# Moving the issue of six stores per chunk from SyncE to ScalarE in a fused convolution, state-space and mixture-of-experts kernel

## The chip, the cores and the metric

The kernel runs on one core of one Trainium2 chip. The time is device microseconds for one execution of the whole program; the lower the better. Six engines share the work: TensorE (PE, with PEld for its weight loads), VectorE (DVE), ScalarE (ACT), GpSimd (POOL) and SyncE (SP). In the kernel before, SP does nothing but issue transfers. All engines run their own instruction streams in order and meet at semaphores.

## The reference

The input is eight images of 56 x 56 tokens with 64 channels.

```python
# 1. a convolution in 32 paths of width 4
h = relu(bn1(x @ W1 + B1)); h = relu(bn2(conv3x3(h, W2) + B2)); h = relu(bn3(h @ W3 + B3))
x = relu(h.sum(paths) + x);  t = tokens(x)
# 2. a state-space layer over the tokens, forwards and backwards
s = layernorm(t);  xn = layernorm(s) * gamma + beta
#    for each direction:
xs, z = split(xn @ in_proj); xs = silu(conv4(xs)); dt = softplus(xs @ x_proj @ dt_proj + b)
h[t] = exp(dt * A) * h[t-1] + dt * B * xs;  y = (C . h + D * xs) * silu(z) @ out_proj
t = t + s + y_fwd + y_bwd
# 3. eight experts, the best two of each token, of a 64-256-64 MLP
s = layernorm(t);  t = t + moe(s, top_k=2)
```

## The kernel before

**Tiling.** An image is cut into seven chunks of 448 tokens (eight rows). The state-space layer takes each chunk twice, once in each direction, so an image has 14 steps. A step has 16 slots, one for each state (DS = 16), and the whole kernel is one loop over slots n on every engine. In slot n, PE spreads the n-th input of the recurrence into a bank (line 683), VectorE weighs it by B and runs the scan (lines 1008, 1018), GpSimd multiplies by C (line 1172), and PE gathers (line 695). ScalarE makes the decays `dtb` by an Exp (dA, line 854), up to six slots ahead (AHEAD = 6); the first of a step waits for the transfer that spreads `dt` over the partitions.

**Order.** The other two layers are woven into these slots by tables of offsets. The convolution of a chunk has a slot CONV and stages at offsets of A_AT and F_AT; the experts of a chunk have a slot TOKENS and offsets of E_AT. For all images but the first, CONV is 8 modulo 16 and comes every 32 slots, that is every second step. On each engine the order of a slot is fixed by the order of its loop body. PE and its evictors share two banks in a ring; ScalarE takes most of them in `take`.

**The chain of the step size dt.** GpSimd finishes softplus in `soft_dt` (line 1193). SP stores the result in `put_dt` (line 543, slot 5 of the step) and reads it back spread over the partitions in four transfers `spread_dt` (line 550), of which the first waits for the store. The scan of the next step needs them.

**The six stores.** `keep_rows` (line 584) stores a chunk of the first layer's rows; `put` (line 604) stores the second layer's output as three bf16 parts, one call each; `keep_xn` (line 620) stores the normed tokens in two calls. That makes one, three and two issues, six per chunk and 336 for all 56 chunks. The load `arrange` (line 613, three transfers) reads all three parts back as `h3` and must wait until they have landed (semaphore `bounced`). What is stored is made by ScalarE: `h1s` at line 869, the first part at 875, the other two in `split_h2` at 937, `xns` at 888.

**Where the slots fall.** With CONV = 8 modulo 16, the second layer is evicted and its first part stored in slot 14 of a step; in the next step part two is split in slot 1 and stored in slot 2, part three is split in slot 3 and stored in slot 4, and `arrange` also stands in slot 4, ahead of `put_dt` in slot 5. `keep_xn` of the chunk before stands in slot 1. The experts' first layer ("up", Gelu, line 896) fills slots 8 to 11 of one step and 0 to 3 of the next. In those slots ScalarE makes no decays, so that the activation table isn't changed; it makes up for them in the slot after:

```python
if not bursting and not silu:
    decays_to(n + AHEAD)      # first in the slot's body
```

Of the kernel before, what the change touches and what calls it, by code (L numbers as in the profile page):

```python
# [19 lines left out]
ROWS = 8  # L20
# [39 lines left out]
END = NB * G  # L60
DOWN_AT = (4, 7, 12, 15)
PAIR_AT = (4, 6, 12, 13)
A_AT = {"cut": -16, "second": -11, "put0": -10, "rem1": -10, "split1": -7, "put1": -6, "rem2": -8,
        "split2": -5, "put2": -4, "arrange": -4, "z": 6, "x_in": 10, "paths": 14, "mean": 15, "square": 17, "var": 17,
# [17 lines left out]
def build(nc, T):  # L82
    ctx = ExitStack()
    with ctx:
# [335 lines left out]
        def first_half(k):  # L420
            return 0 <= k + 2 < LAST

        def second_half(k):
            return 0 <= k + 1 < LAST
# [15 lines left out]
        for r in range(NB):  # L440
            for q in range(NCH):
                for what, at in A_AT.items():
                    slots["A", what, (r, q)] = G * r + CONV[a_class(r)][q] + at
                for what, at in F_AT.items():
                    slots["A", what, (r, q)] = G * r + ROWS_IN[a_class(r)][q] + at
                for j in range(ZP):
                    slots["A", "third", ((r, q), j)] = G * r + CONV[a_class(r)][q] + j * 11 // ZP
                for m in range(len(ACT_J) + 1):
                    slots["A", "z_T", ((r, q), m)] = G * r + CONV[a_class(r)][q] + A_AT["z"] + m
                t = G * r + TOKENS[e_class(r)][q]  # L450
                for what, at in E_AT.items():
                    slots["E", what, (r, q)] = t + at
                for m in range(MT):
                    slots["E", "up", ((r, q), m)] = t + EXPERTS + (m // 2 if m < 8 else 4 + m // 2)
# [31 lines left out]
        RING += [(DS * k + 11, 1, "z", k + 1, "act") for k in range(-1, LAST - 1)]  # L486
# [20 lines left out]
        for k in range(-2, LAST):  # L507
            if second_half(k):
                MISC += [(DS * k + 4, "bb", k + 1), (DS * k + 6, "cc", k + 1)]
            if first_half(k):  # L510
                MISC += [(DS * k + 12, "x", k + 2), (DS * k + 15, "dt", k + 2)]
# [26 lines left out]
        with nc.Block() as block:  # L538
            @block.sync
            def _(sp_):  # L540
# [40 lines left out]
                def keep_rows(it):  # L581
                    after(r_act, taken("paths_in", it))
                    a = (1 + F_ORD[it[1]] * ROWS) * PW
                    sp_.dma_start(h1_dram[:, a:a + ROWS * PW], h1s[:, :, :].rearrange("p r w -> p (r w)"))\
                       .then_inc(h1_out, 16)

# [11 lines left out]
                def put(it, a):  # L598
                    if a == 0:
                        after(r_act, taken("second", it))  # L600
                        after(h3_in, 48 * upto("A", "arrange", back(it, 2)))
                    else:
                        after(h2_mid, upto("A", "split1", it) + upto("A", "split2", it if a == 2 else back(it)))
                    sp_.dma_start(T["h2_scratch"][side(it), a].rearrange("c t n -> t c n"), h2p[:, a, :])\
                       .then_inc(bounced, 16)

# [9 lines left out]
                def keep_xn(it):  # L616
                    after(r_act, taken("norm_T", it))
                    for h in range(2):
                        at = A_ORD[it[1]] * CH + 3 - h
                        sp_.dma_start(xn_dram[it[0] % 2][C * h:C * h + C, at:at + CH],  # L620
                                      xns[C * h:C * h + C, :]).then_inc(xn_out, 16)

# [6 lines left out]
                for n in SLOTS:  # L629
                    k, i = n // DS, n % DS  # L630
                    if i == 4 and first_half(k):
                        fetch_xw(k + 2)
                    if i == 5 and second_half(k):
                        put_dt(k + 1)
                    for j in range(3):
                        if i == (7, 9, 13)[j] and second_half(k):
                            spread_dt(k + 1, j)
                    if i == 1 and 0 <= k < LAST:
                        spread_dt(k, 3)
# [28 lines left out]
            def _(pe):  # L668
# [16 lines left out]

                def gather_y(b):
                    k, j = b // 4, b % 4
                    if j == 0:
                        if k:
                            pe.wait_ge(o_rd, k)  # L690
                        MM(ps[YB][:, 0:CH], skip[k % 2][:, :], u[:, k % 2, :], start=True, stop=False,
                           skip_group_check=True)
# [128 lines left out]
                for n in SLOTS:  # L821
                    k, i = n // DS, n % DS
# [6 lines left out]
                    if i == 3 and 1 <= k <= LAST:  # L829
                        gather_y(4 * k - 1)  # L830
                    if i == 6 and 1 <= k <= LAST:
                        out_proj(k - 1)
                    if i in (9, 11, 15) and 0 <= k < LAST:
                        gather_y(4 * k + (9, 11, 15).index(i))
# [6 lines left out]
            def _(act):  # L841
# [19 lines left out]
                def take(what, of):  # L861
# [15 lines left out]
                    elif what == "third":  # L877
                        it, j = of
                        n, m = len(ACT_J), ACT_J.index(j)
                        gg = (upto("A", "z", it) - 1) * n + m - 4  # L880
# [23 lines left out]
                    last.then_inc(r_act, 1)  # L904

# [48 lines left out]
                for n in SLOTS:  # L954
                    k, i = n // DS, n % DS
                    bursting = any(n - ago in starts for ago in range(4))
                    silu = i == 12 and (first_half(k) or second_half(k))
# [8 lines left out]
                    if silu and first_half(k):  # L966
                        silu_u(k + 2)
# [13 lines left out]
                    if i == 5 and second_half(k):  # L981
                        copy_bb(k + 1)
                    if i == 7 and second_half(k):
                        copy_cc(k + 1)
                    if i == 15 and first_half(k):
                        soft_in(k + 2)

            @block.vector
            def _(dve):
# [42 lines left out]
                def rectify(it, j):  # L1032
                    m, a = DVE_J.index(j), acc[:, :]
                    z = bank_of("third", (it, j))[:, 0:CH]
                    if m == 0:
                        after(z_T, (len(ACT_J) + 1) * (upto("A", "z", it) - 1))
# [7 lines left out]
                def paths_out(it):  # L1044
# [3 lines left out]
                    dve.wait_ge(z_T, (len(ACT_J) + 1) * upto("A", "z", it))  # L1048
# [64 lines left out]
                for n in SLOTS:  # L1113
                    k, i = n // DS, n % DS
# [4 lines left out]
                    if i == 3 and 1 <= k <= LAST:  # L1119
                        gate(k - 1)  # L1120
                    if i == 6 and 1 <= k <= LAST:
                        add_out(k - 1)
# [29 lines left out]
            def _(pool):  # L1152
# [119 lines left out]
                for n in SLOTS:  # L1272
                    k, i = n // DS, n % DS
                    if 0 <= n < END:
                        by_c(n)
                        if i % 2 == 1:
                            keep_states(n)
                    if second_half(k):
                        if i == 0:
                            soft_le(k + 1)  # L1280
                        if i == 1:
                            soft_ym(k + 1)
                        if i == 2:
                            soft_log(k + 1)
                        if i == 3:
                            soft_dt(k + 1)
                        if i in (4, 5, 6):
                            part(k + 1, i - 4)
# [104 lines left out]
```

## Time and profile before

| | |
|---|---|
| median of 3 runs | 5047.22 us (5043.57 to 5048.93) |
| profiled execution | 5048.39 us, span 5046.6 us |
| busy: PE, DVE, POOL, ACT | 4298.5, 4019.9, 3923.8, 3319.4 us |
| bytes moved by DMA | 623.07 MB, mean 123 GB/s |
| granted TensorE clock, mean | 0.953 |

The span is from the first to the last instruction; the execution's own time is 1.8 us longer. No engine is busy all the time; the share of each is an average over slots with different limits.

### The profile page before, as it was taken

The numbers are of one execution on the slowest core, as the hardware profiler recorded it, in microseconds if no ns is written. First come the engines' busy times: TensorE is split into PE (matmuls) and PEld (weight loads), VectorE is DVE, ScalarE is ACT, GpSimd is POOL, SyncE is SP. The second block draws the span as 40 slices with busy tenths as digits, with TensorE's granted clock in tenths as the row PEclk, the third lists the DMA queues.
The fourth block names the chain that finished last, engine by engine and source line by source line (L and its number), as shares of the span: only waits on it lengthen the run. The fifth ranks groups of instructions, "written<-read, shape, count | busy, mean of one in ns | idle before, by whom it ended". The sixth has DMA issues, their size and how long they took to land.

```text
span 5046.6 us, 70047 instructions
## 1 busy us (share of the span) xinstructions
PE 4298.5 (85%) x21206; PEld 1758.3 (35%) x21206; DVE 4019.9 (80%) x6065; ACT 3319.4 (66%) x5396; POOL 3923.8 (78%) x4938
## 2 busy tenths in 40 slices
PE   3577788889898888888889898989898889888887
PEld 1233333333333333333333333333333333332332
DVE  2278888788887888888888888888888888888772
ACT  1265566667676667777776777767676767676675
POOL 1277788788887788888887888888888888888872
PEclk8688999999999999999999999999999999999998
DMA  2275655555555555555555555555555556554430
GB/s 66 66 163 135 142 131 129 134 129 134 126 132 125 130 132 129 132 137 130 139 128 134 132 136 131 132 134 133 131 137 131 131 129 136 133 123 110 98 75 5
DMA packets 255531, 623.07 MB, mean 123 GB/s; under 512 B 105268, under 2 KB 170676, under 8 KB 255028
## 3 DMA queue, kind: packets, MB, share of 16 engines
q1 hardware_dynamic: 255156, 618.60, 52.9%
q8 instruction: 171, 2.80, 0.3%
q14 instruction: 204, 1.67, 0.1%
HBM read 540.85 MB, written 77.65 MB: 123 GB/s over the span
## 4 chain that ended last, share of the span: by engine, by line
PE 33%; ACT 16%; POOL 16%; DVE 12%; issue 11%; DMA 10%; DVEq 0%; SPq 0%; ACTq 0%; POOLq 0%
PE ps L683 7%; POOL hc L1172 6%; ACT dtb L854 6%; DVE hs L1018 5%; DMA dtb<-dt_scratch 5%; PE ps L746 5%; PE ps L695 4%; DVE ps L1008 4%; DMA dt_scratch<-sp 3%; ACT L969 3%; PE ps L817 2%; PE ps L740 2%; ACT hg L896 2%; POOL sp L1185 2%; PE ps L772 2%
## 5 line engine op out<-in xcount | busy, mean ns | idle before, releaser
L1172 POOL TENSOR_TENSOR hc<-hs,cb 128x448 f32<-128x448 f32 x1792 | 2031.3, 1137 | 644.7 <-DVE hs L1018 620.6
L1018 DVE TENSOR_TENSOR_SCAN hs<-dtb,state,ps 128x448 f32<-128x448 f32 x1536 | 1755.1, 1143 | 91.2 <-DVE ps L1008 2.0
L1008 DVE TENSOR_TENSOR ps<-ps,bb 128x448 f32<-128x448 f32 x1792 | 1098.9, 613 | 427.7 <-PE ps L683 420.8
L854 ACT ACTIVATE dtb<-dtb,decay 128x448 f32<-128x448 f32 x1792 | 1087.6, 658 | 190.6 <-DMA dtb<-dt_scratch 189.2
L683 PE MATMUL ps<-dux,pick 128*128 128x448 bf16 x3584 | 1039.3, 371 | 113.0 <-DVE hs L1018 107.7
L896 ACT ACTIVATE hg<-ps,be 128x448 f32<-128x448 f32 x896 | 519.4, 631 | 411.3 <-PE ps L746 409.8
L683 PE MATMUL ps<-duz,pick 128*128 128x448 bf16 x1792 | 642.5, 359 | 0.0
L746 PE MATMUL ps<-xn,we 64*128 64x448 f32 x1792 | 564.1, 596 | 32.2 <-ACT hg L896 31.7
L683 PEld LDWEIGHTS ps<-dux,pick 128*128 128x128 bf16 x3584 | 264.5, 99 | 797.7 <-issue 459.7
L730 PE MATMUL ps<-h,w 96*128 96x448 bf16 x896 | 313.9, 386 | 196.6 <-ACT rz L885 72.1
L695 PE MATMUL ps<-hc,gather 128*32 128x448 f32 x3584 | 451.8, 577 | 0.8 <-POOL hc L1172 0.6
L885 ACT ACTIVATE rz<-ps,bnb 128x448 f32<-128x448 f32 x448 | 280.8, 627 | 214.8 <-PE ps L806 108.9
L1040 DVE SCALAR_TENSOR_TENSOR acc<-ps,nb,acc 128x448 f32<-128x448 f32 x392 | 265.9, 678 | 179.2 <-PE ps L730 179.1
L817 PE MATMUL ps<-hg,we 128*64 128x448 f32 x1792 | 392.5, 559 | 18.3 <-ACT rz L903 10.6
L1018 DVE TENSOR_TENSOR_SCAN hs<-dtb,zeros,ps 128x448 f32<-128x448 f32 x256 | 292.5, 1142 | 13.9
L806 PE MATMUL ps<-ident,rz 128*112 128x128 f32 x1792 | 293.6, 290 | 0.0
L969 ACT ACT_TABLE_LOAD x225 | 288.7, 1283 | 4.0
L746 PEld LDWEIGHTS ps<-xn,we 64*128 64x128 f32 x1792 | 198.0, 187 | 244.4 <-ACT hg L896 144.6
L806 PEld LDWEIGHTS ps<-ident,rz 128*112 128x112 f32 x1792 | 225.2, 141 | 139.0 <-issue 107.3
L683 PEld LDWEIGHTS ps<-duz,pick 128*128 128x128 bf16 x1792 | 175.5, 98 | 191.8 <-issue 16.7
L1269 POOL TENSOR_TENSOR yw<-yw 128x448 f32<-128x448 f32 x168 | 190.3, 1133 | 45.3 <-DVE yw L1103 45.1
L730 PEld LDWEIGHTS ps<-h,w 96*128 96x128 bf16 x896 | 83.8, 101 | 404.8 <-ACT rz L885 138.3
(176 smaller groups left out, 6362.6 us busy)
## 6 DMA issues: line engine op xcount, KB each, us to landing
dtb<-dt_scratch SPq DMA_DIRECT2D x448, 896.0 KB, 6.5
slab<-h_scratch SPq DMA_DIRECT2D x168, 290.0 KB, 8.0
dt_scratch<-sp SPq DMA_DIRECT2D x112, 224.0 KB, 2.0
h_scratch<-h2p SPq DMA_DIRECT2D x168, 112.0 KB
h<-h_scratch SPq DMA_DIRECT2D x56, 336.0 KB, 4.2
h_scratch<-h1s SPq DMA_DIRECT2D x56, 232.0 KB, 4.1
xw<-xn_scratch SPq DMA_DIRECT2D x112, 112.8 KB, 2.6
xw<-xn_scratch SPq DMA_DIRECT2D x112, 112.5 KB, 2.7
```

The lines of the kernel that those rows point to most:

```text
L683: last = MM(ps[BU[n % 3]][:, 0:CH], pick[:, i, :], part, start=(a == 0), stop=(a == 2))
L695: last = MM(ps[YB][32 * q:32 * q + 32, 0:CH], gather[:, 24 - 8 * j:56 - 8 * j], hc[:, (4 * b + q) % 8, :], start=False, stop=(j == 3), ski ...
L730: last = MM(out[:, 0:CH], w3[:, j // 2, 2 * (j % 2):2 * (j % 2) + 2, :].rearrange("p a b -> p (a b)"), h3[:, j // 2, :], start=True, stop= ...
L746: last = MM(out[:, 0:CH], we1[half, m, :], xn2[half, side(it), :], start=True, stop=True)
L806: last = MM(ps[AB][0:TT, j * 128:(j + 1) * 128], src[:, j * TT:(j + 1) * TT], ident[:, :], is_transpose=True, start=(m == 0 and j == 0), s ...
L817: last = MM(ps[AB][C * h:C * h + C, 0:CH], we2[:, ORDER[g], :], hg[:, g % 8, :], start=(g % 4 < 2), stop=(g % 4 >= 2))
L854: A.activation(a, a, ACT.Exp, scale=decay[k % 2][:, i:i + 1]).then_inc(a_ok, 1)
L896: last = A.activation(hg[:, g % 8, :], out[:, 0:CH], ACT.Gelu, bias=be1[:, m:m + 1])
L969: A.preload_act_table_set("natural_log_exp_and_others")
L1008: V.tensor_tensor(bank, bank, bb[:, k % 2, :], ALU.mult).then_inc(bu_ok, 1)
L1018: V.tensor_tensor_scan(rev(hs[:, n % RH, :], d), rev(dtb[i // 4][:, i % 4, :], d), rev(bank, d), state[:, d, i:i + 1] if k % STEPS >= 2 el ...
L1172: P_.tensor_tensor(hc[:, n % 8, :], hs[:, n % RH, :], cb[:, k % 2, :], ALU.mult).then_inc(hc_ok, 1)
```

## The change

The functions `keep_rows`, `put` and `keep_xn` move from SP's program to ScalarE's, with their waits as they were, and are called in ScalarE's loop behind the evictions, the decays and `split_h2` of the slot. SP keeps all else. The other edits of the diff write the slots of the steps as a table (STEP_AT and its like) with the same values, so each other engine's instructions and their order stay as they were: for example `put_dt` has the offset -11, which is slot 5 of the step before. The core of the diff:

```diff
@@ @block.sync
-                def keep_rows(it):
-                    ...
-                def put(it, a):
-                    ...
-                def keep_xn(it):
-                    ...
@@ loop of SP
-                    for it in now("A", "rows", n):
-                        keep_rows(it)
-                    for a in range(3):
-                        for it in now("A", ("put0", "put1", "put2")[a], n):
-                            put(it, a)
-                    for it in now("A", "keep_xn", n):
-                        keep_xn(it)
@@ @block.scalar
+                def keep_rows(it):
+                    after(r_act, taken("paths_in", it))
+                    a = (1 + F_ORD[it[1]] * ROWS) * PW
+                    act.dma_start(h1_dram[:, a:a + ROWS * PW], h1s[:, :, :].rearrange("p r w -> p (r w)"))\
+                       .then_inc(h1_out, 16)
+
+                def put(it, a):
+                    if a == 0:
+                        after(r_act, taken("second", it))
+                        after(h3_in, 48 * upto("A", "arrange", back(it, 2)))
+                    else:
+                        after(h2_mid, upto("A", "split1", it) + upto("A", "split2", it if a == 2 else back(it)))
+                    act.dma_start(T["h2_scratch"][side(it), a].rearrange("c t n -> t c n"), h2p[:, a, :])\
+                       .then_inc(bounced, 16)
+
+                def keep_xn(it):
+                    after(r_act, taken("norm_T", it))
+                    for h in range(2):
+                        at = A_ORD[it[1]] * CH + 3 - h
+                        act.dma_start(xn_dram[it[0] % 2][C * h:C * h + C, at:at + CH],
+                                      xns[C * h:C * h + C, :]).then_inc(xn_out, 16)
@@ loop of ScalarE, behind the decays, take, silu_u and this:
                     for a in (1, 2):
                         for it in now("A", ("", "split1", "split2")[a], n):
                             split_h2(it, a)
+                    for it in now("A", "rows", n):
+                        keep_rows(it)
+                    for a in range(3):
+                        for it in now("A", ("put0", "put1", "put2")[a], n):
+                            put(it, a)
+                    for it in now("A", "keep_xn", n):
+                        keep_xn(it)
```

## Rows read from the trace of the kernel before

**Rows 1.** The page's first part: busy time, share of the span, instructions of each engine.

```profile
PE 4298.5 (85%) x21206; PEld 1758.3 (35%) x21206; DVE 4019.9 (80%) x6065; ACT 3319.4 (66%) x5396; POOL 3923.8 (78%) x4938
```

**Rows 2.** The chain that ended last, whole span, shares by engine and line.

```profile
by line: issue 10.9%; PE ps L683 7.3%; POOL hc L1172 5.7%; ACT dtb L854 5.5%; DVE hs L1018 5.5%; DMA dtb<-dt_scratch 5.2%; PE ps L746 4.7%; PE ps L695 4.3%; DVE ps L1008 4.2%; DMA dt_scratch<-sp 3.4%; ACT L969 2.6%; PE ps L817 2.2%; PE ps L
```

**Rows 3.** The chain in order of time, 2225 to 2300 us: start, duration, what.

```profile
2281.44 1.10 POOL sp L1189
...
2283.77 1.10 POOL sp L1193
2284.89 4.20 DMA dt_scratch<-sp
2289.11 6.76 DMA dtb<-dt_scratch
...
2297.03 0.62 ACT rz L885
```

**Rows 4.** SP's timeline in 2262 to 2300 us: start, duration, what it issued.

```profile
2266.72 0.62 SPq L604 DMA_DIRECT2D h_scratch<-h2p  x1
2268.94 0.52 SPq L550 DMA_DIRECT2D dtb<-dt_scratch  x1
2270.58 1.12 SPq L620 DMA_DIRECT2D xn_scratch<-xns  x2
2275.26 0.62 SPq L604 DMA_DIRECT2D h_scratch<-h2p  x1
...
2280.58 0.63 SPq L604 DMA_DIRECT2D h_scratch<-h2p  x1
2283.19 1.25 SPq L613 DMA_DIRECT2D h<-h_scratch  x3
2284.89 0.34 SPq L543 DMA_DIRECT2D dt_scratch<-sp  x1
```

**Rows 5.** SP's own waits, whole span: us in total, times, longest.

```profile
SPq L604 <- ACT h2p L875: 393.3, 56, 15.4
SPq L543 <- POOL sp L1193: 366.3, 109, 14.0
...
SPq L604 <- ACT h2p L937: 338.9, 106, 6.8
SPq L550 <- DMA dt_scratch<-sp: 283.6, 112, 4.5
```

**Rows 6.** ACT's timeline in 2262 to 2300 us; in brackets its idle time before.

```profile
2265.99 0.71 ACT L875 ACTIVATE h2p<-ps,bnb,bng 128x448 bf16<-128x448 f32 x1
2266.59 0.66 ACT L854 ACTIVATE dtb<-dtb,decay 128x448 f32<-128x448 f32 x1
...
2274.67 0.57 ACT L937 ACTIVATE h2p<-h 128x448 bf16<-128x448 f32 x1
2275.77 1.16 ACT L896 ACTIVATE hg<-ps,be 128x448 f32<-128x448 f32 x2 [0.54 <-PE ps L746]
...
2279.98 0.58 ACT L937 ACTIVATE h2p<-h 128x448 bf16<-128x448 f32 x1
2280.47 3.45 ACT L854 ACTIVATE dtb<-dtb,decay 128x448 f32<-128x448 f32 x6
...
2295.89 1.23 ACT L854 ACTIVATE dtb<-dtb,decay 128x448 f32<-128x448 f32 x2 [3.31 <-DMA dtb<-dt_scratch]
```

**Rows 7.** Lines 604, 620 and 584: duration of an issue in ns, min/median/max.

```profile
L604 SPq DMA_DIRECT2D h_scratch<-h2p x168: 570/627/680, 95.2 to 4443.5; - x168
...
L620 SPq DMA_DIRECT2D xn_scratch<-xns x112: 445/588/642, 152.7 to 4514.5; - x112
...
L584 SPq DMA_DIRECT2D h_scratch<-h1s x56: 325/344/1894, 64.7 to 4233.9; - x56
```

**Rows 8.** All waits of the whole span, the one for the spread dt.

```profile
ACT dtb L854 <- DMA dtb<-dt_scratch: 189.2, 57, 10.5
```

**Rows 9.** DMA issues: count, KB each, median us from issue to landing.

```profile
dt_scratch<-sp SPq DMA_DIRECT2D x112, 224.0 KB, 2.0
```

**Rows 10.** SP's timeline 900 us later, in 3170 to 3215 us.

```profile
3194.20 0.63 SPq L604 DMA_DIRECT2D h_scratch<-h2p  x1
3196.79 1.25 SPq L613 DMA_DIRECT2D h<-h_scratch  x3
3198.51 0.34 SPq L543 DMA_DIRECT2D dt_scratch<-sp  x1
```

More of the change, by code:

```diff
@@ L60 @@
 END = NB * G
+STEP_AT = {"fetch_xw": -28, "x": -20, "silu_u": -20, "dt": -17, "soft_in": -17, "bb": -12, "copy_bb": -11,
+           "cc": -10, "copy_cc": -9, "z": -5, "soft_le": -16, "soft_ym": -15, "soft_log": -14, "soft_dt": -13,
+           "part0": -12, "part1": -11, "part2": -10, "put_dt": -11, "spread0": -9, "spread1": -7, "spread2": -3,
+           "spread3": 1, "skip": 9, "gather0": 9, "gather1": 11, "gather2": 15, "gather3": 19, "gate": 19,
+           "out_proj": 22, "add_out": 22}
+UP_AT = [m // 2 if m < 8 else 4 + m // 2 for m in range(16)]
 DOWN_AT = (4, 7, 12, 15)
 PAIR_AT = (4, 6, 12, 13)
+THIRD_AT = [j * 11 // 16 for j in range(16)]
+FOLD_AT = [6 + m for m in range(9)]
 A_AT = {"cut": -16, "second": -11, "put0": -10, "rem1": -10, "split1": -7, "put1": -6, "rem2": -8,
-        "split2": -5, "put2": -4, "arrange": -4, "z": 6, "x_in": 10, "paths": 14, "mean": 15, "square": 17, "var": 17,
+        "split2": -5, "put2": -4, "arrange": -4, "x_in": 10, "paths": 14, "mean": 15, "square": 17, "var": 17,
         "power": 17, "scaled": 18, "normed": 19, "norm_T": 23, "keep_xn": 25}
@@ L418, in e_class, with steps_at @@
             return "mid" if r < NB - 1 else "last"
[L420 to L424, printed above, removed]
+        def steps_at(n, *whats):
+            for what in whats:
+                kk, i = divmod(n - STEP_AT[what], DS)
+                if i == 0 and 0 <= kk < LAST:
+                    yield kk
         def side(it):
@@ L446, in build @@
                 for j in range(ZP):
-                    slots["A", "third", ((r, q), j)] = G * r + CONV[a_class(r)][q] + j * 11 // ZP
+                    slots["A", "third", ((r, q), j)] = G * r + CONV[a_class(r)][q] + THIRD_AT[j]
                 for m in range(len(ACT_J) + 1):
-                    slots["A", "z_T", ((r, q), m)] = G * r + CONV[a_class(r)][q] + A_AT["z"] + m
+                    slots["A", "z_T", ((r, q), m)] = G * r + CONV[a_class(r)][q] + FOLD_AT[m]
                 t = G * r + TOKENS[e_class(r)][q]
@@ L453, in build @@
                 for m in range(MT):
-                    slots["E", "up", ((r, q), m)] = t + EXPERTS + (m // 2 if m < 8 else 4 + m // 2)
+                    slots["E", "up", ((r, q), m)] = t + EXPERTS + UP_AT[m]
                 for i in range(PAIRS):
@@ L485, in build @@
             RING += [(slots["E", what, of], rank, what, of, "act") for of in of_stage["E", what]]
-        RING += [(DS * k + 11, 1, "z", k + 1, "act") for k in range(-1, LAST - 1)]
+        RING += [(DS * k + STEP_AT["z"], 1, "z", k, "act") for k in range(LAST)]
         RING = sorted(RING, key=lambda job: job[0:2])
@@ L506, in build @@
         MISC = []
[L507 to L511, printed above, removed]
+        for k in range(LAST):
+            MISC += [(DS * k + STEP_AT[what], what, k) for what in ("x", "dt", "bb", "cc")]
         for what in ("tokens_T", "logits", "fold"):
@@ L579, in fetch_res @@
                        .then_inc(rs_in[side(it)], 16)
-                def keep_rows(it):
[L582 to L585, printed above, removed]
                 def cut_slab(it):
@@ L596, in cut_slab @@
                            .then_inc(slab_in, 16)
-                def put(it, a):
[L599 to L605, printed above, removed]
                 def arrange(it):
@@ L614, in arrange @@
                         row += 16 * parts
-                def keep_xn(it):
[L617 to L621, printed above, removed]
                 def put_out(it):
@@ L629, in _ @@
                 for n in SLOTS:
[L630 to L639, printed above, removed]
+                    for kk in steps_at(n, "fetch_xw"):
+                        fetch_xw(kk)
+                    for kk in steps_at(n, "put_dt"):
+                        put_dt(kk)
+                    for j in range(4):
+                        for kk in steps_at(n, ("spread0", "spread1", "spread2", "spread3")[j]):
+                            spread_dt(kk, j)
                     for it in now("A", "fetch", n):
                         fetch_x(it)
-                    for it in now("A", "rows", n):
-                        keep_rows(it)
                     for it in now("A", "cut", n):
                         cut_slab(it)
-                    for a in range(3):
-                        for it in now("A", ("put0", "put1", "put2")[a], n):
-                            put(it, a)
                     for it in now("A", "arrange", n):
@@ L684, in pick_du, with skip_y @@
                     last.then_inc(bu_ps, 1)
+                def skip_y(k):
+                    if k:
+                        pe.wait_ge(o_rd, k)
+                    MM(ps[YB][:, 0:CH], skip[k % 2][:, :], u[:, k % 2, :], start=True, stop=False,
+                       skip_group_check=True)
                 def gather_y(b):
                     k, j = b // 4, b % 4
[L688 to L692, printed above, removed]
                     pe.wait_ge(hc_ok, 4 * b + 4)
@@ L821, in _ @@
                 for n in SLOTS:
-                    k, i = n // DS, n % DS
                     if 0 <= n < END:
@@ L828, in _ @@
                         ring_job(q)
[L829 to L834, printed above, removed]
+                    for kk in steps_at(n, "skip"):
+                        skip_y(kk)
+                    for j in range(4):
+                        for kk in steps_at(n, ("gather0", "gather1", "gather2", "gather3")[j]):
+                            gather_y(4 * kk + j)
+                    for kk in steps_at(n, "out_proj"):
+                        out_proj(kk)
                     for it, m in now("A", "z_T", n):
@@ L879, in take @@
                         n, m = len(ACT_J), ACT_J.index(j)
-                        gg = (upto("A", "z", it) - 1) * n + m - 4
+                        gg = (upto("A", "paths", it) - 1) * n + m - 4
                         if gg >= 0:
@@ L954, in _ @@
                 for n in SLOTS:
-                    k, i = n // DS, n % DS
                     bursting = any(n - ago in starts for ago in range(4))
-                    silu = i == 12 and (first_half(k) or second_half(k))
+                    silu = bool(list(steps_at(n, "silu_u")) + list(steps_at(n - 1, "z")))
                     if not bursting and not silu:
@@ L965, in _ @@
                             take(what, of)
-                    if silu and first_half(k):
-                        silu_u(k + 2)
+                    for kk in steps_at(n, "silu_u"):
+                        silu_u(kk)
                     if silu or n - 3 in starts:
@@ L980, in _ @@
                         weigh(it)
[L981 to L986, printed above, removed]
+                    for kk in steps_at(n, "copy_bb"):
+                        copy_bb(kk)
+                    for kk in steps_at(n, "copy_cc"):
+                        copy_cc(kk)
+                    for kk in steps_at(n, "soft_in"):
+                        soft_in(kk)
             @block.vector
@@ L1035, in rectify @@
                     if m == 0:
-                        after(z_T, (len(ACT_J) + 1) * (upto("A", "z", it) - 1))
+                        after(z_T, (len(ACT_J) + 1) * (upto("A", "paths", it) - 1))
                     dve.wait_ge(r_ps, made("third", (it, j)))
@@ L1047, in paths_out @@
                     after(rs_in[side(it)], 16 * upto_side("A", "x_in", it))
-                    dve.wait_ge(z_T, (len(ACT_J) + 1) * upto("A", "z", it))
+                    dve.wait_ge(z_T, (len(ACT_J) + 1) * upto("A", "paths", it))
                     link(V.tensor_tensor(tmp[:, 0], b3[:, :, 0:C], x, ALU.add))
@@ L1113, in _ @@
                 for n in SLOTS:
-                    k, i = n // DS, n % DS
                     if 0 <= n < END:
@@ L1118, in _ @@
                         weigh_b(n + 1)
[L1119 to L1122, printed above, removed]
+                    for kk in steps_at(n, "gate"):
+                        gate(kk)
+                    for kk in steps_at(n, "add_out"):
+                        add_out(kk)
                     for it, j in now("A", "third", n + 1):
@@ L1272, in _ @@
                 for n in SLOTS:
-                    k, i = n // DS, n % DS
                     if 0 <= n < END:
                         by_c(n)
-                        if i % 2 == 1:
+                        if n % 2 == 1:
                             keep_states(n)
[L1278 to L1288, printed above, removed]
+                    for kk in steps_at(n, "soft_le"):
+                        soft_le(kk)
+                    for kk in steps_at(n, "soft_ym"):
+                        soft_ym(kk)
+                    for kk in steps_at(n, "soft_log"):
+                        soft_log(kk)
+                    for kk in steps_at(n, "soft_dt"):
+                        soft_dt(kk)
+                    for a in range(3):
+                        for kk in steps_at(n, ("part0", "part1", "part2")[a]):
+                            part(kk, a)
                     for a in (1, 2):
```

## The prediction

> **What bounds the kernel now.** I read the page's shares first: no engine is full, PE 85%, DVE 80%, POOL 78%, ACT 66% [rows 1]. So the order and the waits set the time, and the view to read is the chain that ended last. Its shares are spread over all engines, and two entries matter here: the store of dt (3.4% of the span) and its spread load (5.2%) [rows 2]. In order of time, that piece is GpSimd's last softplus operation, which ends at 2284.87, SP's store of dt at 2284.89, its landing 4.20 us later, 6.76 us for the first spread load, and then ScalarE's evictions [rows 3]. The wait view agrees: ScalarE stood 189.2 us, in 57 waits, for the spread load [rows 8]. So once in nearly every chunk (32 slots, some 80 us) everything hangs on when SP issues the store of dt.
>
> Then I read SP, which loses the six issues. By its own waits it stands before the dt store waiting for GpSimd in 109 of 112 cases, and before the first spread load in all 112 [rows 5]. SP is early for both; its waits at line 604 (393.3 and 338.9 us) hold back nothing on the chain. In the timeline the order at this place is: third part at 2280.58, h3 load at 2283.19 (it waits for the third part to land), its three issues until 2284.44, store of dt at 2284.89 [rows 4]. Only 0.45 us lie between the end of the h3 issues and the dt store. The same two distances, 2.6 and 1.7 us, come back 900 us later [rows 10]. The h3 load stands ahead of the dt store in SP's order, and the diff leaves that so.
>
> **The change part by part.** *Removed from SP:* 56 x 0.344 + 168 x 0.627 + 112 x 0.588 = 190 us of issues and the waits before them [rows 7]. As SP waits for others before both dt transfers [rows 5], I price that at nothing; what hides it is GpSimd's softplus and the store's landing. Bound of a gain: the third part could leave no earlier, since SP issues it at 2280.58, when ScalarE has just written it (2279.98 + 0.58) [rows 4, 6].
>
> *Added to ScalarE:* the same 190 us, if an issue costs there what it costs SP; ScalarE issues nothing now, so the trace has no row for it. From below an issue can hide behind the activation that ScalarE is just executing (0.6 us), from above it adds whole. What matters is where these stand.
>
> *The third part (the main term).* Its split at 2279.98 is in slot 3, its store in slot 4. ScalarE makes no decays during the experts' burst, and begins slot 4 with the decays owed: the run of six at 2280.47, 3.45 us, of which five are slot 4's and the last is slot 5's [rows 6]. They start (3.45 - 0.66) / 5 = 0.56 us apart. So the store stands where the sixth decay began, at 2280.47 + 5 x 0.56 = 2283.3, in place of 2280.58: 2.7 us late. If the queue can pass it on right behind the start of the fifth it is 2.2, if at its end 2.8.
>
> *What pushes ScalarE before that.* The first part's store waits for ScalarE's own eviction, which ends at 2266.70, then takes 0.62; the next decay began at 2266.59, so it is 0.73 late. The two stores of the normed tokens (1.12 together) stand behind the split at 2274.67, and the second part's store (0.62) one slot on; the next Gelus had 0.54 us of idle before them [rows 4, 6]. If the issues run beside the activation ahead of them, they add about 0.1 to 0.2 each time, if not, 0.6. A part of the first 0.73 may vanish in the idle of the burst. I take 1.0 in all, bounds 0.3 and 1.9. The third part is then issued 3.7 us late (2.5 to 4.7).
>
> *What is late next.* The h3 load waits for it, 2.61 us from issue to issue [rows 4]: 2284.3 + 2.6 = 2286.9. Its three issues take 1.25, and the dt store behind them goes at 2288.2, 3.3 us later than at 2284.89; 0.45 us of slack was there and is used up. GpSimd's end at 2284.87 no longer decides, even if it moves by the 1 us that ScalarE is late. The landing: the dt store took 4.20 us here [rows 3] but 2.0 in the median [rows 9]; what distinguishes this place is the h3 load of 672 KB just ahead. If that load sets it, dt lands 2289.11 - 2283.19 = 5.92 us after the h3 load starts, at 2292.8, 3.7 late; by its own 4.20 it is 3.3 late. I take 3.5 per chunk; bounds 2.05 (2.5 less 0.45) and 4.65 (4.7 less 0.45 and 0.4 more for the landing).
>
> *How often.* 3.4% of 5046.6 us by 4.20 makes 41 passages of the chain through the dt store, 5.2% by 6.76 makes 39 through the spread load [rows 2, 3]: I take 39. The burst with its owed decays exists for 45 chunks (not for the first image's seven nor the next four, which come before any expert). For the six chunks between 39 and 45 the chain goes elsewhere, but ScalarE waits for the spread there too (57 waits, 3.3 us in the mean [rows 8]), so I count half: 39 x 3.5 + 6 x 1.7 = 147 us. In the other eleven chunks one decay stands before the store, not five; up to 1 us each, 5 us in all at most. The rows' store (0.34 us) follows an eviction off this place; I add 3 us for it. Sum 150 us. On the profiled execution: 5046.6 + 150 = 5197 of span, 5198 with the 1.8 us around it; that execution is 1.2 us above the median. I say 5200.
>
> *A rule weighed.* The rows put the store's landing here at 4.20 us and elsewhere at 2.0 [rows 3, 9]. The Trainium skill, page "DMA: Bandwidth & Descriptors", section "Issuing engines are not separate DMA queues", says that issuing from several engines saves only the sequencer's time for initiating a transfer, which is usually small. By that rule this change frees 190 us of SP and gives back nothing else, which would make the time the same if SP's order were all that moved. The trace agrees that SP has no need of it; the rule is silent on what the engine that takes over is late with.
>
> **The rivals.**
> *Absorbed.* The dt store is 2 to 3 us late, but half is won back behind it, because GpSimd and VectorE use the pause to work off their backlog. For it: GpSimd is busy 78% and follows closely. Against: the chain runs straight through the landing into ScalarE's evictions (2295.89 to 2297.03) [rows 3, 6]. It gives 39 x 1.5 = 60 to 80 us: 5105 to 5125.
> *ScalarE pays each issue in full.* The six issues (0.34 + 3 x 0.63 + 2 x 0.59 = 3.4 us a chunk) all lengthen the ring of PE and ScalarE beside the late dt store: 45 x (3.5 + 2.5) = 270 us, since 1.0 of them is in the 3.5: 5317. Against it are the idle times in the burst [rows 6].
> *The other side: the parts land sooner.* On a queue of ScalarE's own the third part doesn't follow SP's transfers. If it were issued as early as now and landed in 2.0 us as the dt store mostly does, not 2.6, the h3 load would start 0.6 us sooner and, if that load is what makes dt land late, so would dt: 39 x 0.6 = 23 us, 5024. It decides if ScalarE reaches the store before 2280.6; the five owed decays stand against it.
> *Nothing changes.* If the spread load had slack of 3.5 us before ScalarE's evictions, the delay would be hidden. ScalarE's 3.31 us of idle before the decay [rows 6] speak against it.
>
> **How the numbers follow.** 0.2% is about what a measurement of this kernel can tell from no change. The late third part, as summed: 0.63, with its own range 39 x 2.05 = 80 to 45 x 4.65 = 209 us, 5127 to 5256. Absorbed 0.14. Each issue in full 0.13. Sooner landing 0.06. Nothing 0.04. Faster 0.06, same 0.04, slower 0.90. The range takes in most of the absorbed case and reaches to the lower part of the full one: 5105 to 5300.
>
> **What would show it.** The third part's store on ScalarE behind five decays and some 3.7 us after its place in the cycle now; the h3 load 2.6 us behind it; the dt store at once behind the h3 issues, no longer waiting for GpSimd at this step; ScalarE's waits for the spread load well above 189 us, near 189 + 150; the share of the dt store and its spread in the chain not smaller, and the chain going through lines 604 and 613 of before in place of GpSimd's softplus. I am wrong if ScalarE passes the store on ahead of the decays, if an issue costs ScalarE far more or less than the 0.62 us of SP, or if two engines that issue at once slow each other down.

## The result: 0.6% slower, a fifth of what was forecast

The changed kernel took 5074.82 us (median of 7 runs, 5062.31 to 5090.31) against 5043.57 us (7 runs, 5038.25 to 5049.35). The ratio is 1.0063, with a 95% interval of 1.0049 to 1.0077: 31 us slower, where 153 were forecast, and outside the range. The profiled execution is the slowest of the seven, 5090.31 us with a span of 5088.5; I use its rows for the order and the length of single steps, and the medians for the loss.

The page of the changed kernel, its list of DMA queues: the stores now go through a queue of their own, q10.

```profile
q1 hardware_dynamic: 215284, 573.17, 50.1%
q10 hardware_dynamic: 39872, 45.43, 3.3%
```

The first thing to look at is the third part's store, which the forecast had 3.7 us late. ScalarE's timeline of one chunk of the changed kernel, with its DMA issues as ACTq (start, duration, what; idle time before in brackets):

```profile
2361.28 0.71 ACT L849 ACTIVATE h2p<-ps,bnb,bng 128x448 bf16<-128x448 f32 x1
2362.03 0.58 ACTq L892 DMA_DIRECT2D h_scratch<-h2p  x1
2362.66 0.67 ACT L828 ACTIVATE dtb<-dtb,decay 128x448 f32<-128x448 f32 x1 [0.66 <-ACT h2p L849]
...
2370.22 0.50 ACTq L899 DMA_DIRECT2D xn_scratch<-xns  x1
2370.22 0.63 ACT L870 ACTIVATE hg<-ps,be 128x448 f32<-128x448 f32 x1
2370.74 0.57 ACT L933 ACTIVATE h2p<-h 128x448 bf16<-128x448 f32 x1
2370.75 0.61 ACTq L899 DMA_DIRECT2D xn_scratch<-xns  x1
2371.84 0.63 ACT L870 ACTIVATE hg<-ps,be 128x448 f32<-128x448 f32 x1 [0.54 <-PE ps L720]
2371.95 0.63 ACTq L892 DMA_DIRECT2D h_scratch<-h2p  x1
...
2376.05 0.58 ACT L933 ACTIVATE h2p<-h 128x448 bf16<-128x448 f32 x1
2376.54 0.65 ACT L828 ACTIVATE dtb<-dtb,decay 128x448 f32<-128x448 f32 x1
2376.66 0.61 ACTq L892 DMA_DIRECT2D h_scratch<-h2p  x1
2377.10 2.90 ACT L828 ACTIVATE dtb<-dtb,decay 128x448 f32<-128x448 f32 x5
```

The split of part three ends at 2376.63 and its store is issued at 2376.66, while the first of the owed decays runs and four more that precede the store in the program have not begun. The decays follow at their old spacing (2376.54, 2377.10), as if nothing stood between them. The normed tokens' first store goes out at 2370.22, ahead of the split (2370.74) that precedes it in the program, and the Gelu behind them still waits 0.54 us for PE, as in [rows 6]. So ScalarE's queue hands activations to the engine ahead of time and then works on the issue beside them. The Trainium skill describes this in "Perfetto Trace Analysis", section "Per-instruction lifecycle: what the profiler-reported window actually captures": an activation is pushed into a wait queue and the sequencer is ready for the next instruction, while a DMA instruction holds the sequencer itself from its semaphore wait until its descriptors are made. The rows agree in both halves. The second half shows in the first part's store: it waits for the eviction of 2361.28 (end 2361.99), nothing has been handed over behind it, and the engine stands idle for 0.66 us until the issue is done.

SP's timeline for the same chunk:

```profile
2379.24 1.26 SPq L603 DMA_DIRECT2D h<-h_scratch  x3
2380.97 0.34 SPq L548 DMA_DIRECT2D dt_scratch<-sp  x1
```

The distances are those of before: third part to h3 load 2.58 us (2.61 in [rows 4]), h3 load to dt store 1.73 (1.70). SP still waits for GpSimd before the dt store: 111 of 112 times, 109 before [rows 5]. What moved is the eviction to dt store distance: 2380.97 - 2361.99 = 18.98 us, against 2284.89 - 2266.70 = 18.19 in [rows 4, 6], 0.79 longer. The waits of the whole span in the changed kernel (us in total, times, longest) and, in a second fence, of the kernel before:

```profile
ACT dtb L828 <- DMA dtb<-dt_scratch: 191.5, 57, 10.8
...
POOL h L1213 <- ACT h2p L933: 71.9, 48, 7.2
...
ACT dtb L828 <- ACT h2p L849: 34.8, 52, 0.7
```

```profile
POOL h L1212 <- ACT h2p L937: 32.5, 43, 7.2
```

There is one new wait, 34.8 us in 52 chunks, and one that grew by 39.4 us: GpSimd's remainder (what is left of `h` when a bf16 part is taken off), waiting for ScalarE's split of part two. That operation stands in GpSimd's order between the softplus steps that lead to the dt store. GpSimd's rows of the same two chunks show it, first the changed kernel, then the kernel before:

```profile
2369.01 1.13 POOL L1182 TENSOR_TENSOR sp<-sp 128x448 f32<-128x448 f32 x1
2371.39 1.03 POOL L1213 TENSOR_TENSOR h<-h,h2p 128x448 f32<-128x448 f32 x1 [1.25 <-ACT h2p L933]
```

```profile
2273.71 1.32 POOL L1181 TENSOR_TENSOR sp<-sp 128x448 f32<-128x448 f32 x1
2275.31 1.03 POOL L1212 TENSOR_TENSOR h<-h,h2p 128x448 f32<-128x448 f32 x1 [0.29 <-ACT h2p L937]
```

Counted from the end of the first part's eviction, the first softplus step starts as before (7.02 against 7.01 us), the remainder behind it starts 0.79 us later (9.40 against 8.61), and from there to the dt store it is 9.58 us in both kernels. So GpSimd loses the 0.79 us at this one wait and hands it on whole. ScalarE's wait for the spread dt, which was to grow by 150 us, went from 189.2 [rows 8] to 191.5.

### The profile page after: what moved, and what is told of

Its sections match the earlier page's. It is cut to its first block, busy times and chain, and to the rows that moved or that the text cites. A ratio compares the mean times of both kernels' runs of the same rounds, so it can differ in the third digit from the quotient of the medians.

```text
span 5088.5 us, 70047 instructions
## 1 busy us (share of the span) xinstructions
PE 4349.7 (85%) x21206; PEld 1772.0 (35%) x21206; DVE 4041.3 (79%) x6065; ACT 3325.4 (65%) x5396; POOL 3916.9 (77%) x4938
## 4 chain that ended last, share of the span: by engine, by line
PE 34%; ACT 16%; POOL 15%; DVE 12%; issue 11%; DMA 10%; DVEq 0%; ACTq 0%; SPq 0%; POOLq 0%
PE ps L656 7%; ACT dtb L828 6%; POOL hc L1173 5%; DMA dtb<-dt_scratch 5%; DVE hs L1020 5%; PE ps L720 5%; PE ps L669 4%; DVE ps L1010 4%; DMA dt_scratch<-sp 3%; ACT L964 3%; PE ps L714 2%; PE ps L791 2%; ACT hg L870 2%; POOL sp L1186 2%; PE ps L751 2%
## 5 line engine op out<-in xcount | busy, mean ns | idle before, releaser
L828 ACT ACTIVATE dtb<-dtb,decay 128x448 f32<-128x448 f32 x1792 | 1089.2, 658 | 231.0 <-DMA dtb<-dt_scratch 191.5
L720 PE MATMUL ps<-xn,we 64*128 64x448 f32 x1792 | 596.0, 597 | 33.1 <-ACT hg L870 32.7
L1213 POOL TENSOR_TENSOR h<-h,h2p 128x448 f32<-128x448 f32 x112 | 116.1, 1037 | 172.1 <-ACT h2p L849 100.1
```

What stands on the lines that cost most here:

```text
L720: last = MM(out[:, 0:CH], we1[half, m, :], xn2[half, side(it), :], start=True, stop=True)
L828: A.activation(a, a, ACT.Exp, scale=decay[k % 2][:, i:i + 1]).then_inc(a_ok, 1)
```

## The experiments

The changed kernel's functions are meant where `act` issues; "before" is the kernel before.

**Which of the six issues costs.** First alone, then all others. The first-part-alone kernel:

```diff
 # before, only this store moved to ScalarE's loop
+                    for it in now("A", "put0", n):
+                        put(it, 0)
```

> The kernel before with one edit: only the first part's store (56 of the 336 issues) is issued by ScalarE; the rest stay on SP. Theory A (the whole cost is the 0.78 us per chunk in which ScalarE's queue stands for its own eviction, 2361.99 us, and then for the issue of the first part's store until 2362.61, so that the next decay starts at 2362.66 and not at 2361.88): the same loss as the whole change, 25 to 40 us over before. Theory B (two queues at once, or the number of issues, cost the time): a sixth of it, about 5 us. Theory of the prediction (the third part is late): nothing, since the third part is on SP here.

Measured: 5087.15 us against 5046.06, ratio 1.0079 (1.0062 to 1.0096). The whole loss is there with 56 of 336 issues, and the third part on SP. TensorE's granted clock is no rival for it: its mean is 0.953 to 0.955 in the five executions of this kernel, 0.950 to 0.958 in the seven of the changed kernel and 0.950 to 0.957 in those of the kernel before.

```diff
 # the changed kernel, the first part's store back on SP
-                    for a in range(3):
+                    for a in (1, 2):
```

> The changed kernel with one edit back: the first part's store is on SP again, the other 280 issues stay on ScalarE. Theory A: the loss is gone, within 8 us of before. Theory B: five sixths of the loss stay, about 26 us over before. Theory of the prediction: nearly all of it stays, since the third part's store is on ScalarE. The trace should show the third part's store right behind the split (0.03 us after its end), ahead of most of the owed decays.

Measured: 5042.40 us against 5046.06, ratio 0.998 (0.9964 to 0.9996). The loss is gone, and a gain of 0.2% shows (0.04 to 0.36%). Its ScalarE timeline has the third part's store where the changed kernel has it, with the five decays after it:

```profile
2262.14 0.65 ACT L853 ACTIVATE dtb<-dtb,decay 128x448 f32<-128x448 f32 x1
2262.27 0.62 ACTq L917 DMA_DIRECT2D h_scratch<-h2p  x1
2262.70 2.89 ACT L853 ACTIVATE dtb<-dtb,decay 128x448 f32<-128x448 f32 x5
```

280 issues on ScalarE cost nothing in time here, and neither does a second queue.

**The store one slot on.** The first part's store behind work that doesn't wait for it:

```diff
-                    for a in range(3):            # in slot n, right behind the eviction
+                    for a in (1, 2):
...
+                    for it in now("A", "put0", n - 1):   # a slot later, behind the decays and take
+                        put(it, 0)
                     for kk in steps_at(n, "silu_u"):
```

> The changed kernel with the first part's store called one slot on in ScalarE's program, behind a decay and the eviction of line 877, which don't depend on it. Theory A: the queue hands these two to the engine before it waits for the store, the engine has 1.1 us of work meanwhile, and the idle time of 0.66 us after the second eviction is gone: within 8 us of before, with the parts and the h3 load where they were. Theory B: no change against the changed kernel, about 31 us over before.

Measured: 5041.36 us against 5046.06, ratio 0.9994 (0.998 to 1.0007). All six issues are on ScalarE and nothing is lost. Its timeline:

```profile
2257.41 0.71 ACT L849 ACTIVATE h2p<-ps,bnb,bng 128x448 bf16<-128x448 f32 x1
2258.02 0.66 ACT L828 ACTIVATE dtb<-dtb,decay 128x448 f32<-128x448 f32 x1
2258.16 0.59 ACTq L892 DMA_DIRECT2D h_scratch<-h2p  x1
2258.58 0.53 ACT L877 ACTIVATE rz<-ps 128x448 f32<-128x448 f32 x1
```

The store leaves at 2258.16, 0.04 us after the eviction's end, as early as on SP, though a decay and an eviction stand before it in the program; and both run on without a gap.

**The wait and the issue apart.**

```diff
 # before, all stores on SP; ScalarE, behind take() of that slot
+                    for it in now("A", "put0", n):
+                        after(r_act, taken("second", it))
```

> The kernel before, all stores on SP, with one wait added in ScalarE's program: after the second layer's eviction it waits for that eviction to end, and issues nothing. It parts the 0.78 us per chunk of theory A into the wait and the issue. If the wait alone costs: what is lost is the overlap of two activations (0.10 us) and the restart (0.03 us), 0.1 to 0.2 us a chunk, 5 to 10 us over before, and the issue is the larger part. Rival: the wait drains more than that (0.5 us or more a chunk): over 20 us.

Measured: 5044.28 us against 5036.71, ratio 1.0016 (1.0004 to 1.0028), about 8 us (2 to 14). In the trace the eviction begins at 2260.61 and ends at 2261.32; the decay starts at 2261.35, where, without the wait, it would have started 0.61 us after the eviction's start, at 2261.22. That is 0.13 us a chunk:

```profile
2260.61 0.71 ACT L875 ACTIVATE h2p<-ps,bnb,bng 128x448 bf16<-128x448 f32 x1
2261.35 0.67 ACT L854 ACTIVATE dtb<-dtb,decay 128x448 f32<-128x448 f32 x1
```

**The suspected cost larger.** The first part's store in two halves of the partitions (the counts that others wait for on `bounced` are raised to match, not shown):

```diff
+                    for t in ((0, ZT // 2), (ZT // 2, ZT)) if a == 0 else ((0, ZT),):
+                        act.dma_start(dst[t[0]:t[1]], h2p[16 * t[0]:16 * t[1], a, :]).then_inc(bounced, 16)
```

> The changed kernel with the first part's store cut into two stores of half the partitions, both on ScalarE at the same place. Theory A: ScalarE stands for two issues in place of one; if half the partitions take half the time it is the same 31 us over before, if an issue of half the size takes 0.35 us or more each, 0.1 us or more a chunk longer, so 36 to 60 us over before; what the trace shows as idle time of the next decay times 52 chunks is the size of the step. Theory B (the count of issues): 56 more on 336, about 5 us more.

Measured: 5089.08 us against 5036.71, ratio 1.0108 (1.0088 to 1.0127). The two issues take 1.12 us together, so half the size costs nearly as much as the whole, and ScalarE's idle time before the decay is 1.19 us:

```profile
2355.26 1.12 ACTq L894 DMA_DIRECT2D h_scratch<-h2p  x2
2356.42 0.67 ACT L828 ACTIVATE dtb<-dtb,decay 128x448 f32<-128x448 f32 x1 [1.19 <-issue]
```

The loss grows with the delay. The decay starts 0.13, 0.78 and about 0.78 + 0.53 = 1.31 us late in a chunk. The idle time is in 52 chunks, but only the 45 behind the first eleven lose time by it: the eviction of the twelfth chunk starts at 737.60 us in the changed kernel and at 740.05 us before, that of the last at 4470.71 and 4428.94. Times 45 the three delays are 6, 35 and 59 us; the medians gave 8, 31 (41 with the first part alone) and 52. In the median over these 45 chunks the dt store stands 0.15, 0.79 and 1.33 us later behind the first part's eviction than before, so the delay arrives there whole each time.

**The forecast's late store, made real.** SP's third part waits until the owed decays are done; ScalarE is left alone.

```diff
 # before, in put() on SP
+                    if a == 2:
+                        after(a_ok, min(slots["A", "put2", it] + AHEAD, END - 1) + 1)
```

> The kernel before with one wait added on SP: the third part's store waits until the decays owed at slot 4 are done, that is where the prediction had put it; ScalarE is not touched. If the second half of the prediction was right (store 2.8 us late, 0.45 us of slack, h3 load and behind it the dt store 2.4 us late, on the chain in some 45 chunks): 80 to 125 us over before. Rival: the delay is absorbed behind the dt store (GpSimd and VectorE catch up, as in the prediction's absorbed case): under 50 us. A rival of no effect at all: under 10 us.

Measured: 5243.73 us against 5046.06, ratio 1.0401 (1.0381 to 1.0422): 202 us by the ratio, more than expected. Its SP timeline:

```profile
2345.21 0.63 SPq L606 DMA_DIRECT2D h_scratch<-h2p  x1
2347.78 1.25 SPq L615 DMA_DIRECT2D h<-h_scratch  x3
2349.08 0.42 SPq L543 DMA_DIRECT2D dt_scratch<-sp  x1
2353.95 1.20 SPq L550 DMA_DIRECT2D dtb<-dt_scratch  x2
```

The split ended at 2342.34, so the store is 2.87 us late, the h3 load follows by 2.57, and the dt store stands right behind its issues (SP waits for GpSimd only 66 times now). The dt store landed after 4.87 us, 0.67 more than in [rows 3]. It follows the load more closely here, 1.30 us in place of 1.70; that this is the reason is not shown, since in the chunk of the changed kernel it took 4.55 us with the distance as before. From the split's end to that landing are 11.61 us, against 2289.11 - 2280.56 = 8.55: 3.06 late. The rest is in the time behind it. From ScalarE's decay on the spread dt to its eviction of `u` it took 2368.54 - 2360.68 = 7.86 us, in the changed kernel 2312.80 - 2306.57 = 6.23. The two kernels by stretch (busy us and count of PE, PEld, DVE, ACT and POOL, then the granted clock, DMA share, GB/s), first this kernel, then the kernel before, lined up on the same work:

```profile
2355.00:2361.00 6.00, 5.92 (x28) 2.31 (x27) 4.97 (x8) 0.32 (x1) 6.00 (x7) 0.77 1.00 222
2361.00:2365.00 4.00, 2.52 (x13) 0.71 (x14) 2.87 (x5) 3.51 (x6) 3.44 (x5) 0.95 0.79 158
2365.00:2369.00 4.00, 4.00 (x11) 1.94 (x10) 0.90 (x2) 0.83 (x2) 1.07 (x4) 0.63 0.99 224
```

```profile
2290.00:2296.00 6.00, 4.96 (x31) 2.40 (x31) 4.41 (x7) 1.18 (x3) 6.00 (x8) 1.00 0.97 214
2296.00:2300.00 4.00, 3.53 (x19) 1.13 (x19) 3.96 (x7) 3.53 (x5) 4.00 (x5) 1.00 0.85 167
2300.00:2304.00 4.00, 4.00 (x16) 1.65 (x14) 2.61 (x5) 2.43 (x4) 3.73 (x7) 1.00 0.62 152
```

With the late store the clock granted to TensorE falls to 0.77 and 0.63 of full speed in these stretches, a part of them at 1.2 GHz, where before it stayed at 1.00 (2.4 GHz). The two pairs of matmuls that ScalarE waits for there took 0.91 and 0.92 us before and take 1.70 and 1.31 now:

```profile
2365.70 1.70 PE L774 MATMUL ps<-xw,wx 128*128 128x448 f32 x2
2367.19 1.31 PE L775 MATMUL ps<-xw,wx 128*128 128x448 f32 x2
```

3.06 + 1.63 = 4.7 us a chunk, times 45 chunks is 211 us, against 202 measured. This takes the chunk shown for all. The clock falls in some chunks of every kernel (the changed kernel has 0.71 in 2396 to 2400 us, in the chunk shown above), but more often here: between 700 and 4500 us its mean is 0.95 in this kernel and 0.98 before.

**How far the queue runs ahead.** The third part's store two slots later in ScalarE's program:

```diff
-        "split2": -5, "put2": -4,
+        "split2": -5, "put2": -2,
```

> The changed kernel with the third part's store called two slots later in ScalarE's program (offset -2, slot 6), behind eight more instructions, two or three of which wait for banks of PE. It asks how far the queue runs ahead of the engine. If it runs ahead of any number of instructions that wait for nothing unfulfilled, but not of one that waits: the store is issued about when the copy of B starts (4 us after the split ends), h3 and dt stores late by 3 to 4 us, 100 to 200 us over before. If it runs ahead without limit: the store stays at the split's end, and the time is that of the changed kernel (31 us over before).

Measured: 5290.08 us against 5036.71, ratio 1.0505 (1.0486 to 1.0525). The loss, some 253 us, is above the range of the first case; it holds the changed kernel's own 31. ScalarE's timeline:

```profile
2357.64 0.58 ACT L933 ACTIVATE h2p<-h 128x448 bf16<-128x448 f32 x1
2358.13 3.45 ACT L828 ACTIVATE dtb<-dtb,decay 128x448 f32<-128x448 f32 x6
2360.96 0.62 ACTq L892 DMA_DIRECT2D h_scratch<-h2p  x1
2361.48 0.52 ACT L877 ACTIVATE rz<-ps 128x448 f32<-128x448 f32 x1
2361.91 0.52 ACT L923 ACTIVATE bb<-ps 128x448 f32<-128x448 f32 x1
2362.33 0.66 ACT L828 ACTIVATE dtb<-dtb,decay 128x448 f32<-128x448 f32 x1
2362.89 0.53 ACT L877 ACTIVATE rz<-ps 128x448 f32<-128x448 f32 x1
```

The store is issued 2.74 us after the split's end (2358.22), when the last of six decays has just begun, and four instructions that precede it in the program still lie ahead. In the changed kernel there were also four left when it went out (the run behind 2377.10 has five decays, the last of them the next slot's). The run-ahead is bounded. Whether by a depth of four or by an activation that waited for its bank, these rows don't tell.

**Which way the 0.78 us reaches the end.** GpSimd's remainder one slot later, so that it works on softplus while the split is late, in the kernel before as a control and in the changed kernel:

```diff
-        "rem2": -8,
+        "rem2": -7,
```

> The kernel before with one table entry changed: GpSimd's second remainder (line 1212, which waits for ScalarE's split of part two) is called one slot later, behind the softplus operation of line 1185 and not ahead of it. It is the control for the next kernel. GpSimd no longer stands in front of it (0.29 us a chunk, 32.5 us in all with the first image), but the second split starts some 0.3 us later. Expected: within 15 us of before, rather faster.

Measured: 5083.17 us against 5035.12, ratio 1.009 (1.0064 to 1.0116). The expectation missed: 48 us slower. The remainder ends at 2388.38, the split of part three starts at 2388.41 behind it, and the dt store now stands right behind the h3 load's issues, 1.33 us behind the load's start, where it had 1.70:

```profile
2389.01 0.63 SPq L604 DMA_DIRECT2D h_scratch<-h2p  x1
2391.59 1.25 SPq L613 DMA_DIRECT2D h<-h_scratch  x3
2392.92 0.39 SPq L543 DMA_DIRECT2D dt_scratch<-sp  x1
```

That does not explain the loss. Counted from the first part's store (2375.07 here), the dt store goes 0.32 us sooner than in [rows 4] and lands 0.35 us later, which is 16 us in 45 chunks. The mean granted clock is lower too, 0.944 to 0.949 in the six executions against 0.949 to 0.957 before. Which of these, or what else, makes the 48 us is open.

> The changed kernel with the same table entry. Theory A1 (the 0.78 us reaches the end through GpSimd: split late, remainder late, softplus late, dt store late): GpSimd does other work while the split is late, and the loss against the control is mostly gone, under 12 us. Theory A2 (it reaches the end through the ring of PE and ScalarE, the Gelus of the burst being 0.78 us late): the loss of 25 to 40 us against the control stays.

Measured: 5096.43 us against 5035.12, ratio 1.0113 (1.0094 to 1.0132), 13 us above the control where the change alone costs 31. The intervals of the two kernels overlap, and the loss lies between what the two theories said. Nor could the pair tell them apart: in its trace the h3 load is late as well (2384.44 - 2367.10 = 17.34 us behind the first part's eviction, 2283.19 - 2266.70 = 16.49 before), and the dt store at 2385.87 stands 0.16 us behind the load's issues. With GpSimd out of the way, the same late splits hold the dt store back through the h3 load. What shows GpSimd's part in the changed kernel is its rows and the unchanged 9.58 us; that the time of the whole kernel is lost by this way alone stays argued.

> The version that the runs point to: all six issues on ScalarE, the first part's store one slot on, and the remainder one slot later. Under A1 and A2 alike it stands with the control, within 10 us; a gain over before of more than 0.2% would have to come from the remainder's move.

Measured: 5075.71 us against 5035.12, ratio 1.0074 (1.0051 to 1.0098). It stands with the control, as expected, and is no gain. No version here beats the median of the kernel before by more than 0.2%.

## Why the prediction was wrong

**What bounds the kernel** was read rightly: SP's issues, and what each waits for, at the h3 load and the dt store. The kernel with the store made late, by a wait on SP alone, shows that this place sets the time.

**SP's six issues removed, priced at nothing:** right. With 280 of the 336 moved the time is 0.998 of before.

**The third part 2.7 us late, with bounds of 2.2 and 2.8 us: the step that failed.** It took the order in the program for the order in time, and put the store where the sixth decay began. It was issued 0.03 us after the split's end, as on SP. The lower end, that the queue passes it on "right behind the start of the fifth", was no lower end: the trace had no row of an issue on ScalarE, and the bound should have gone down to nothing, with a rival for it. The rival in which ScalarE reaches the store before the decays was there, at 0.06, but only as a gain.

**What pushes ScalarE before that, 1.0 us in all:** the first part's store was forecast to make the next decay 0.73 late, and it measured 0.78. The normed tokens and the second part, 0.1 to 0.6 each, measured nothing: from the eviction's start to the split of part three it is 14.77 us in place of 13.99, 0.78 more. This 0.78 accounts for the whole loss (35 us in 45 chunks, 31 and 41 measured); the forecast had it as a side term and let it be swallowed by the h3 load's delay.

**What is late next:** the h3 load did follow by 2.6 us, but from a store that is late by the same 0.79 us as its split and no more. The forecast had the dt store wait for the h3 issues. They end at 2380.50, 0.47 us ahead of it, so it is GpSimd that still decides. The growth of GpSimd's wait for the split (39.4 us) and its rows name the path; the pair of kernels made to test it could not. Without GpSimd's delay the h3 issues would take its place: 0.79 less the 0.45 us of slack is 0.34 us, an estimate.

**How often:** the new idle time needs no burst and shows in 52 chunks. The time is lost in the 45 that the forecast counted, all of it behind the twelfth chunk's eviction.

**The rest of the sum**, tried by itself: a store 2.87 us late brought 202 us, where by the forecast's working (2.87 less 0.45, plus the landing, some 2.5 to 3 us in 39 to 45 chunks) 100 to 135 would come. The landing came 6.17 us after the start of the h3 load, near the forecast's 5.92; the fall of TensorE's granted clock, another 1.6 us in the chunk shown, was missing from the sum. So even with the main term as forecast the size would have been too small.

## What to carry to other kernels

In these runs an issue on a compute engine cost the time in which the queue stood with nothing handed to the engine, and nothing beyond it. Put it behind one or two instructions that don't depend on what is stored, and it goes out as early and for nothing (here the ratio was 0.9994); put it ten activations behind, as the third part two slots on, and it goes out 2.74 us late; put it right behind the instruction that makes the data, with a wait for it, and the engine stands for the wait and the whole issue (here 0.66 us of idle time and 0.78 us of delay a chunk, 31 us in the whole kernel). And before pricing a moved instruction by its place in the program, ask what the queue has handed over by then; without a row of it, the bound goes down to zero.

## What the runs showed that was not expected

ScalarE's issue at a place in the program may leave ahead of up to four activations that stand before it (third part in the changed kernel, and two slots on). An issue of half the partitions takes 0.56 us where the whole takes 0.61: the price is that of the instruction more than of its size. The store of the normed tokens lands in 2.3 us in the median from ScalarE's queue; from SP it took 4.8, behind a spread of dt issued 1.6 us before it [rows 4]. Whether that spread is the reason was not tried, and the kernel gained nothing by it. With a delay of 3 us in a chunk of 80, the clock granted to TensorE fell from 1.00 to 0.77 and 0.63 in stretches of 6 and 4 us behind it, and the delay cost half as much again. PE had waited 1.40 us for GpSimd and 0.42 us for the h3 load; the first wait was there before, 1.39 us, with the clock at 1.00, the second is new.
